# Graph network and routed feed-forward on one core: the order of three steps at the start of the feed-forward part

## What is computed

```python
x = x + gnn(layernorm(x), adj, ...)        # convolution over nodes, message passing, a GRU at the end:
                                           #   (1 - z) * tanh(gi_n + r * gh_n) + z * x
h = layernorm(x)
weights = (einsum('bsd,do->bso', h, wr) + br)[..., 0]
_, idx = top_k(weights, 512)               # per batch
sel_idx = idx[:, :511]                     # the 511 best nodes
sel = take_along_axis(h, sel_idx)
y = (gelu(sel @ w1 + b1) @ w2 + b2) * weights[sel_idx]   # w1: 128 x 512, w2: 512 x 128
x = x + (zeros.at[sel_idx].set(y) + h)
```

## Time and profile before

| | |
|---|---|
| three timed runs | median 562.78 us (562.45 to 562.78) |
| the profiled execution | 561.96 us, of which the span of the trace is 560.1 us |
| busy in the span | PE 544.9 us (97%), DVE 475.0 (85%), ACT 355.2 (63%), POOL 276.1 (49%) |
| mean granted clock of TensorE | 0.999 of full |

### The profile page before, as it was taken

The page is one execution under the profiler, slowest core; times in us unless marked ns, Lnnn a source line. Parts: engine busy times, 40 slices in busy tenths (PEclk is TensorE's granted clock), DMA queues, the critical chain, the costliest instruction groups (busy, mean ns, idle before and its releaser), DMA issues.

```text
span 560.1 us, 9036 instructions
## 1 busy us (share of the span) xinstructions
PE 544.9 (97%) x2964; PEld 414.8 (74%) x2964; DVE 475.0 (85%) x1056; ACT 355.2 (63%) x617; POOL 276.1 (49%) x346
## 2 busy tenths in 40 slices
PE   7899999999999999999999999999999999989996
PEld 4876798678967896689767986798678966755663
DVE  7997388689898989899999989898979987988722
ACT  5867485856586667748674857575856673645552
POOL 3640354325358444834484546654545265437552
PEclk9999999999999999999999999999999999999999
DMA  8703700270008200750057001800171005402102
GB/s 276 280 0 80 297 0 2 71 305 1 2 11 294 109 2 1 208 207 1 1 136 278 1 2 54 323 2 1 46 282 49 1 1 180 160 12 85 38 33 62
DMA packets 33340, 54.53 MB, mean 97 GB/s; under 512 B 2098, under 2 KB 23051, under 8 KB 33166
## 3 DMA queue, kind: packets, MB, share of 16 engines
q1 hardware_dynamic: 29710, 48.42, 24.8%
q0 software_dynamic: 3584, 5.54, 2.9%
HBM read 44.21 MB, written 13.43 MB: 103 GB/s over the span
## 4 chain that ended last, share of the span: by engine, by line
PE 81%; DVE 11%; issue 3%; ACT 3%; POOL 1%; DMA 0%; DVEq 0%; ACTq 0%; POOLq 0%
PE N L1548 19%; PE M L1525 10%; PE C L1381 7%; PE C L1382 6%; PE C L1383 6%; PE D L1519 5%; PE N L1642 4%; PE N L1381 3%; PE N L1382 3%; PE N L1383 3%; ACT hab L681 2%; PE M L1382 2%; PE M L1381 2%; PE M L1383 2%; DVE tr L1036 2%
## 5 line engine op out<-in xcount | busy, mean ns | idle before, releaser
L787 ACT ACTIVATE tr<-D 128x512 f32<-128x512 f32 x128 | 76.4, 597 | 75.6 <-PE D L1519 73.9
L1525 PEld LDWEIGHTS M<-cst,adjb 128*128 128x128 f32 x512 | 63.8, 141 | 35.5 <-issue 20.8
L1519 PE MATMUL D<-V,U 128*128 128x512 f32 x128 | 89.3, 698 | 0.7 <-DVE V L1095 0.7
L1525 PE MATMUL M<-cst,adjb 128*128 128x128 f32 x512 | 76.8, 272 | 0.6 <-DVE ga L1127 0.6
L581 POOL DMA_INDIRECT sel<-R,ridx x56 | 61.1, 1090 | 16.0 <-issue 13.8
L1548 PE MATMUL N<-ga,msgF 128*128 128x512 f32 x128 | 64.2, 593 | 0.0
L1548 PE MATMUL N<-tz,msgF 128*128 128x512 f32 x128 | 64.2, 593 | 0.0
L1381 PE MATMUL C<-zR,wc 128*128 128x256 f32 x208 | 60.6, 291 | 0.1
L1382 PE MATMUL C<-zR,wc 128*128 128x256 f32 x208 | 58.6, 282 | 0.0
L1383 PE MATMUL C<-zR,wc 128*128 128x256 f32 x208 | 58.5, 281 | 0.0
L1157 DVE TENSOR_SCALAR_CACHE_REDUCE junk<-W,R 128x1024 bf16<-128x1024 f32 (+3 forms) x64 | 51.7, 808 | 3.7 <-ACT W L749 3.7
(11 more groups left out here) (245 smaller groups left out, 1523.9 us busy)
## 6 DMA issues: line engine op xcount, KB each, us to landing
adjb<-in_adj SPq DMA_DIRECT2D x8, 4096.0 KB, 14.9
adjb<-sel SPq DMA_DIRECT2D x7, 516.0 KB, 5.3
xall<-in_x SPq DMA_DIRECT2D x7, 512.0 KB, 5.3
out<-R SPq DMA_DIRECT2D x7, 512.0 KB, 3.6
R<-in_conv_w SPq DMA_DIRECT2D x1, 1088.0 KB, 7.1
sel<-R,ridx POOLq DMA_INDIRECT x56, 3.5
xall<-in_weights SPq DMA_DIRECT2D x1, 832.0 KB, 9.8
xall<-in_x SPq DMA_DIRECT2D x2, 256.0 KB, 2.8
```

Source lines behind the costliest of these rows:

```text
L787: nc.scalar.activation(E[:, u % NE, :], Db[u % NH][:, :], ACT.Exp, scale=-1.0).then_inc(exp_ok, 1)
L1519: MM(Db[h][:, :], U[:, t * P:(t + 1) * P], V[:, half(h)], start=True, stop=True).then_inc(d_ps, 1)
L1525: i = TR(Mb[h][:, k * P:(k + 1) * P], adjb[:, h * TH + k, t * P:(t + 1) * P], ident)
```

## The change

Three steps change places; no instruction is added, taken away or changed in size.

- On PE, in group 0, the transpose of group 1 stands ahead of `down(0, 0)`, not behind it.
- On DVE, `blend(7, 1)` stands ahead of `rank(6, 0, 7)` and `indices`, not behind them.
- On DVE, `lo_of_sel(2, 0)` stands behind `state_to_nodes(7)` and ahead of `moments2`; it stood behind `mean_and_variance`.

```diff
                     new_gate(B - 1, 1)
                     rank(B - 2, 0, 6)
                     lo_of_sel(1, 1)
+                    blend(B - 1, 1)
                     rank(B - 2, 0, 7)
                     indices(B - 2, 0, 1)
-                    blend(B - 1, 1)
                     state_to_nodes(B - 1, (M1, N1))
+                    lo_of_sel(2, 0)
                     moments2(B - 1)
                     mean_and_variance(1, stats2, T * B, slice(0, T), NH)
-                elif not last:
+                elif b > 1 and not last:
                     lo_of_sel(b + 1, 1 - q)
...
                         up(b + 1, 1 - q, j - 1)
-                    down(b, q, j)
                     if first and j == 0:
                         sel_to_features(1)
+                    down(b, q, j)
                     if first and j == 1:
                         up(1, 1, 0)
```

## The result

The changed kernel takes 564.35 us (median of 11 runs, 562.76 to 565.83), the kernel before 562.78 us (median of 11, 562.15 to 563.50). The ratio is 1.0027, with a 95% interval of 1.0019 to 1.0036: slower by 1.6 us. The number forecast was 563.3, so most of the loss wasn't in it. The time lies in the range given, just under the rival in which the clock falls (564.5 to 565.7).

The account below looks back on a forecast made before the run. PE was busy 97% of the span, but DVE's serial chain ahead of the row of weights set the time. The chain starting 0.56 us later gave 562.52 profiled, 563.34 by the median; range 562.2 to 564.9.

Parts of the forecast that it names:

- the rival in which the clock falls: PE between 502.45 and 505.99: clock falls in the new pause, 3.0 us slower, 565.7, or 564.5 for half; chance 0.12.
- The first move: Group 1's transpose ahead of down(0, 0): `xTL` starts at 489.07, 0.71 us earlier, and PE's 0.55 us wait goes.
- The blend: Blend ahead of the rank: PE's 0.90 us wait goes, `state_back` starts 1.78 us earlier, at 492.17; `state_to_nodes` ends 1.56 earlier.
- the indices of batch 6: Indices behind the blend come 0.75 us later, at no cost, since POOL takes them only behind its reciprocal root.
- The third move: `lo_of_sel(2, 0)` ahead of the moments: 1.51 us waiting and 0.61 work use up the 1.56 won; moments 0.56 later.
- The shift lasts: No slack between 505.43 and 515.72 or behind it: 0.56 us arrives whole at the kernel's end.
- The clock: PE ahead of the first row of weights: pause of 3.54 us, not 0.46; full clock assumed to hold.
- the tail's fall: Kernel's end before the change: clock fell from full to half some 3.2 us after PE's last matmuls.
- a sign of being wrong: Granted clock below 1.00 in a window between 505 and 511 us would show the forecast wrong.
- the sum: Profiled 561.96 + 0.56 = 562.52; by the median 563.34, or +0.10%.
- The price of the fall: Return to full speed costs up to 2.4 us on PE: first eight matmuls took 5.85 us, against 3.4 later.

## Why the prediction was right in its steps but one, and too low in its number

**The first move: right.** The 0.55 us wait is gone, and `xTL` of group 1 starts as soon as `rank(6, 0, 6)` lets go, with the last accumulator read (489.69) and not behind it. Alone it brings 0.84 us where 0.71 was worked out.

**The blend: right.** `state_back` starts with no bracket, PE being the later one. In the profiled execution it was 492.82 - 0.75 = 492.07, forecast 492.17. Alone it is worth 0.88 us, together with the first 1.6. A slip without effect: the indices of batch 6 come 0.67 us later by the prediction's own numbers (493.06 - 492.39), not 0.75.

**The third move: right, and right in size.** The moments were forecast 0.56 later and came 0.45 to 0.50 later. The difference is there already at up(1, 0), which started at 489.67 (490.42 - 0.75) and not at 489.82: the two down products ahead of it took 1.57 us from start to start and not 1.70. With the pause filled, the whole change costs 0.36 us (the interval goes from 0.1 us less to 0.9 us more than before), and the third move alone 2.3.

**The shift lasts: right.** No slack took it up. The same chain passed on a gain as fully as a loss: with the first two moves it was 1.7 us at the row of weights and 1.6 in the time.

**The clock: wrong.** This is the step that failed. The text had the place, the length of the pause (3.54 us, measured 3.55) and the mechanism, and then took full clock as the likeliest. Its reason was that the tail's fall, 3.2 us after the last matmul, was one case and only 0.3 us shorter than the pause, that the clock stays full through stretches in which PE does little, and that a fall would have to come in most runs. The second reason had little behind it: between its first matmuls and its last, PE's longest stop in that trace is 0.90 us. And the fall does come in most runs; the granted clock below 1.00 between 505 and 511 us, named as a sign of being wrong, is there. Each of the 11 timed runs has a mean granted clock. Two runs have 0.998 and took 562.76 and 563.00 us; the other nine have 0.994 to 0.997 and took 563.99 to 565.83. The mean alone can't tell at 0.997, which traces without a fall in the middle have too (the third move alone, pause filled); the gap of 1 us in the times can. The rival was given 0.12 where it should have been the forecast, and it is no merit of the sum that the time lies in the range: the range held because its upper end was drawn to the middle of this rival. The Trainium skill ("TensorE: Matmul & The Clock Gate", "HAM oscillation — how this bites in real kernels") says that a stall of PE between two bursts of matmuls brings back the half clock and that the next burst starts cold; this case's trace agrees, with 0.50 granted from 506.5 to 509.5.

**The price of the fall: near the upper end at worst, half of it as a rule.** In the profiled execution the fall cost 1.4 us, in the medians 1.2, since the clock was back 2.9 us after PE had resumed; a product's matmuls lie 0.43 us apart there (507.93 to 508.36), not 0.23. The nine runs with a fall took 1.1 to 3.0 us more than the mean of the two without, and in the trace of the third move alone, where the clock came back only 5.5 us after PE had resumed, the fall cost about 2.3 us (its span is 2.5 us above the one with the pause filled, of which 0.2 lie ahead of the row of weights). The prediction read its 2.4 us from PE's first matmuls. The windows there show a granted clock of 1.00, so they don't say that the clock was what made them slow; the weight loads do point that way:

```profile
5.61 0.34 PEld L1598 LDWEIGHTS N<-hab 128*128 128x128 f32 x1 [0.52 <-issue]
6.43 0.19 PEld L1598 LDWEIGHTS N<-hab 128*128 128x128 f32 x1 [0.48 <-issue]
```

One takes 0.34 us at first and 0.19 from 6.43 on, and in the changed kernel one takes 0.33 while 0.50 is granted and 0.19 at 1.00.

## What to carry to other kernels

An instruction that fills a wait of its own engine is free only there. Put ahead of the chain that feeds the wait, it costs its own time and, more, its own wait: here 0.6 and 1.6 us, which ate the 1.7 that the other two moves had won, and more. Look for the instruction that starts the last serial chain, and let nothing wait in front of it. And when PE is made faster ahead of a point where it waits for another engine, work out the pause that this leaves: if a trace shows the clock falling after a stop of that length, even once, at the end, plan with the fall.

## What the runs showed of the hardware

In the middle of a kernel the granted clock fell 2.2 and 3.1 us into a stop of PE, and the falls were irregular. In the changed kernel's profiled execution it fell 3.1 us after the last transposes ended (503.07 to about 506.1) and was back 2.9 us after PE had resumed (506.62 to 509.5). With the third move alone it fell after only 2.2 us (504.81 to 507.0), and was back 5.5 us after PE had resumed (508.35 to 513.8); its times spread from 564.5 to 567.3, and a run took longer the lower its mean granted clock was. Stops of 0.90 us and less, which the kernel before has, left the clock at 1.00. The same pause, filled with twelve matmuls whose result no one reads, made the kernel 1.2 us faster.
